# A three-layer graph convolution on one core: the first projection as fp32 matmuls, and the splits of x moved into hop 1

## The reference, cut to what matters

```python
def _tagconv(x, src, dst, norm, W, b):
    out = x @ W[0]
    h = x
    for k in range(1, K + 1):            # K = 3
        msg = norm[:, None] * h[src]
        h = jax.ops.segment_sum(msg, dst, num_segments=x.shape[0])
        out = out + h @ W[k]
    return out + b

h = jax.nn.relu(_tagconv(x, src, dst, norm, W1, b1))
h = jax.nn.relu(_tagconv(h, src, dst, norm, W2, b2))
out = _layernorm(x + _tagconv(h, src, dst, norm, W3, b3))
```

## Time and profile before

| | |
|---|---|
| median of 3 runs | 1251.7 us (1251.23 to 1251.88) |
| span of the profiled execution | 1250.4 us |
| TensorE busy | 1224.4 us (98%) |
| GpSimd, vector engine, ScalarE busy | 850.6, 629.7, 397.2 us |
| TensorE on the chain that ended last | 88% |
| TensorE matmuls at L1405 | 4104, 944.8 us |

### The profile page before, as it was taken

How to read it: one execution, slowest core, us unless ns; L and a number is a source line. 1 busy time by engine, 2 the same in 40 slices (tenths; PEclk the granted TensorE clock), 3 DMA queues, 4 the chain that set the end, 5 groups by cost and what they waited for, 6 DMA issues and landing times.

```text
span 1250.4 us, 19518 instructions
## 1 busy us (share of the span) xinstructions
PE 1224.4 (98%) x7413; PEld 610.2 (49%) x7413; DVE 629.7 (50%) x1552; ACT 397.2 (32%) x916; POOL 850.6 (68%) x937
## 2 busy tenths in 40 slices
PE   5999999999999999999999999999999999999997
PEld 4655554444444444444444454444444544454444
DVE  7876664444455555433443345555433433345655
ACT  6676774422233331111221122222111111112222
POOL 8677775777477755776577657773777477747773
PEclk8999999999999999999999999999999999999999
DMA  5343443544255553444354435553444344435553
GB/s 182 111 124 107 115 124 101 156 135 135 79 142 157 146 126 104 131 130 125 108 156 132 122 97 150 149 149 94 131 130 128 102 129 130 131 92 151 153 162 93
DMA packets 110070, 160.05 MB, mean 128 GB/s; under 512 B 43719, under 2 KB 82225, under 8 KB 109970
## 3 DMA queue, kind: packets, MB, share of 16 engines
q0 software_dynamic: 40480, 110.54, 31.6%
q1 hardware_dynamic: 69416, 48.13, 12.8%
q10 hardware_dynamic: 74, 0.05, 0.0%
HBM read 120.51 MB, written 32.10 MB: 122 GB/s over the span
## 4 chain that ended last, share of the span: by engine, by line
PE 88%; POOL 5%; DVE 3%; issue 2%; ACT 1%; DMA 1%; POOLq 0%; DVEq 0%; ACTq 0%
PE pb L1405 65%; PE pb L1266 6%; POOL GB L942 4%; PE pb L1319 4%; PE pb L1268 3%; PE pb L1285 3%; PE pb L1161 2%; PE pb L1410 1%; PE pb L1291 1%; PE pb L1383 1%; PE pb L1194 0%; DVE V L1744 0%; POOL gT L825 0%; DMA GB<-vh,KS 0%; DVE gT L1503 0%
## 5 line engine op out<-in xcount | busy, mean ns | idle before, releaser
L942 POOL DMA_INDIRECT GB<-vh,KS x837 | 807.9, 965 | 371.2 <-issue 246.2
L1405 PE MATMUL pb<-V,A 128*128 128x512 f16 x4104 | 944.8, 379 | 0.0
L1405 PEld LDWEIGHTS pb<-V,A 128*128 128x128 fp8e4 x4104 | 395.3, 98 | 429.5 <-issue 5.2
L1789 DVE SCALAR_TENSOR_TENSOR pb<-pb,cst,t 128x256 f32<-128x256 f32 (+1 forms) x200 | 97.7, 488 | 357.8 <-ACT t L1120 357.8
L1120 ACT ACTIVATE t<-pb,cst 128x256 f32<-128x256 f32 (+1 forms) x224 | 105.2, 469 | 441.8 <-PE pb L1410 398.0
L1266 PE MATMUL pb<-Whl,gT 128*128 128x512 f16 x384 | 134.2, 380 | 1.2 <-DVE gT L1730 1.2
L1761 DVE SCALAR_TENSOR_TENSOR V<-V,pb 128x256 f16<-128x256 f16 (+1 forms) x200 | 83.8, 421 | 82.1 <-ACT V L1090 81.5
L1090 ACT ACTIVATE V<-pb 128x256 f16<-128x256 f32 (+1 forms) x200 | 75.9, 383 | 127.3 <-DVE pb L1789 127.2
L1268 PE MATMUL pb<-Whl,gT 128*128 128x256 f16 x384 | 104.7, 273 | 0.0
L1632 DVE TENSOR_REDUCE stat<-V 128x1 f32<-128x256 f16 x225 | 91.3, 412 | 0.2
L1780 DVE TENSOR_REDUCE ast<-A 128x1 f32<-128x610 uint8 x100 | 77.8, 778 | 0.0
(11 more groups left out here) (227 smaller groups left out, 687.8 us busy)
## 6 DMA issues: line engine op xcount, KB each, us to landing
vh<-V SPq DMA_DIRECT2D x216, 128.0 KB
GB<-vh,KS POOLq DMA_INDIRECT x837, 2.8
xr<-in_x SPq DMA_DIRECT2D x24, 128.0 KB, 3.0
out<-g SPq DMA_DIRECT2D x24, 128.0 KB, 1.9
xr<-in_W SPq DMA_DIRECT2D x22, 128.0 KB, 2.4
V<-in_xt SPq DMA_DIRECT2D x5, 512.0 KB, 6.1
gT<-w SPq DMA_TRANSPOSE x46
V<-in_xt SPq DMA_DIRECT2D x1, 640.0 KB, 3.8
```

The source lines that it names most:

```text
L942: pool.indirect_dma_start(GB[:, slot, :], None, vh[vbuf[(L, k + 1)]][:, :], bass.IndirectOffsetOnAxis(ap=KS[:, p:p + 1], axis=0))\
L1405: mm = pe.matmul(acc[:, :], A8[:, a, t * P:(t + 1) * P], src[:, a, :], start=False, stop=(n == NT - 1), skip_group_check=True)
L1789: dve.scalar_tensor_tensor(hi, hi, cst[0:r, 1, t:t + 1], lt, ALU.mult, ALU.add).then_inc(S["s_d1"], 1)
```

## The change

The first projection takes x and W3 as they were loaded, in fp32: two matmuls a tile in place of six. W3's split is gone, and the scale factor SW with it. Eight tiles and not six are projected early; 8 and 9 stand between builds, 10 to 24 are woven into target 0. The splits of x for tiles 0 to 7 stay early; those of tiles 8 to 24 are done one tile at a time, at item `("A", i)` that `split_behind` gives: one tile at i = 1, 4, 5, 6, 8, 10, 11, 13 and 15, and two at 7, 9, 12 and 14. The second keys move to items 1 and 2, their transposes behind dense target 3, their copies to item 5, the tail keys from item 2 to item 6.

```diff
-AHEAD = 9
-BEHIND_P = {6: (4, 5), 7: (6,)}
-KEYED = {("V", 0, 3, 5): 0, ("V", 0, 3, 15): 1}
+AHEAD = 10
+BEHIND_P = {8: (4, 5), 9: (6,)}
...
-SPLITS = {("V", 0, 3, 8): 3, ("V", 0, 3, 11): 4, ("V", 0, 3, 14): 5}
-PAIRED = (6, 6, 2, 2)
+PAIRED = (6, 6, 2, 2, 0, 0, 1, 1)
+XS = 2
+KEYED, KEPT = {1: 0, 2: 1}, 5
...
+def split_behind(i):
+
+    asked = {}
+    for n, it in enumerate(it for it in schedule() if it[0] in "SP" and it[1:3] == (0, 2)):
+        if it[0] == "P" and it[3] in dense(0, 2):
+            at = DENSE.index(it[3])
+            asked.setdefault("next", at + 1)
+            asked["next"] = at + 1
+        elif it[0] == "S":
+            asked[it[3]] = asked.get("next", 0)
+    return [t for t in range(XC[XS], NT) if asked[t] - 2 == i]
...
@@ scalar @@
-            act.activation(Whl[:, 0, :, 3, 0:F], W3, ACT.Copy, scale=SW).then_inc(S["s_whi"], 1)
...
+                    if it[1] == KEPT:
+                        kept(1)
+                    for t in split_behind(it[1]):
+                        x_high(t, t + 1)
@@ tensor @@
-                pe.wait_ge(S["s_xd"], next(c for c in range(len(XC)) if t < XC[c]))
+                pe.wait_ge(s_x[next(c for c in range(len(XC)) if t < XC[c + 1])], 16)
...
                 for c in range(2):
-                    for half, part in ((0, slice(0, F)), (0, slice(F, 512)), (1, slice(0, F))):
-                        mm = pe.matmul(acc, gT[:, t, c, half, 0:r], Whl[:, 0, c, 3, part],
-                                       start=(c == 0 and half == 0 and part.start == 0),
-                                       stop=(c == 1 and half == 1), skip_group_check=True)
+                    at = F * t + P * c
+                    mm = pe.matmul(acc, xT[:, at:at + r], W3[:, c, :], start=(c == 0), stop=(c == 1),
+                                   skip_group_check=True)
...
-            for t in range(6):
+            for t in range(len(PAIRED)):
                 first_projection(t)
...
+                if k == 2:
+                    pe.wait_ge(S["s_xd"], split_at(t))
...
+                if (L, k, t) == (0, 2, DENSE[KEPT - 2]):
+                    swapped(1)
@@ vector @@
-            for c in range(2):
-                x_low(c)
+            for c in range(XS):
+                x_low(XC[c], XC[c + 1])
...
-                    if it[1] == 2:
+                    if it[1] in KEYED:
+                        keyed(1, KEYED[it[1]])
+                    if it[1] == KEPT:
+                        kept(1)
+                    if it[1] == KEPT + 1:
                         tail_keys()
+                    for t in split_behind(it[1]):
+                        x_low(t, t + 1)
```

More of the change, by code:

```diff
@@ L630, in first_acc, with x_part @@
             return bank[bank_of[pe_no[(0, 3, t)]]][0:P if t < NT - 1 else HALF, at:at + F]
-        def x_part(c, half):
-            a, b = XC[c], XC[c + 1]
+        def x_part(a, b, half):
             return (gT[:, a:b, :, half, :], xT[:, F * a:F * b].rearrange("p (t c n) -> p t c n", c=2, n=P))
@@ L641, in bass_tag_gnn_layernorm @@
         names = ("s_h s_w s_b s_cst s_cnt s_idx s_wk s_ki s_kt s_kb s_ka s_hs s_oh s_up s_og s_gc s_vis s_ev "
[L642 removed]
+                 "s_ob s_dw s_pl5 s_rl s_wq s_wi s_deg s_dg s_sq s_cs s_xh s_xd s_pj s_pm s_sm s_c0 s_c5 s_hs64 s_ps s_a1 s_d1 s_a2 "
                  "s_v s_g s_tp s_th s_tl s_z s_ln s_sd s_o s_dd s_st s_ck s_pk s_flag s_turn s_lp "
[L644 removed]
+                 "s_ld s_pl s_at s_at0 s_sg s_dl s_pc s_yg s_yh s_yl s_ps5 s_cp5 s_k5 s_t5 s_s5 s_gm s_nr").split()
         S = {n: sem(n) for n in names}
@@ L950, in _, with x_high @@
             act.activation(lnb[:, 0, 0:1], ones16[:, 0:1], ACT.Sign)
-            act.wait_ge(S["s_w"], 16)
-            act.activation(Whl[:, 0, :, 3, 0:F], W3, ACT.Copy, scale=SW).then_inc(S["s_whi"], 1)
-            def x_high(c):
-                act.wait_ge(s_x[c], 16)
-                if XC[c + 1] > 17:
+            def x_high(a, b):
+                act.wait_ge(s_x[next(c for c in range(len(XC)) if a < XC[c + 1])], 16)
+                if 10 <= a < 16:
                     act.wait_ge(S["s_ki"], QK // KQ)
-                if XC[c + 1] > 21:
                     act.wait_ge(S["s_k5"], 2)
-                high, xs = x_part(c, 0)
+                high, xs = x_part(a, b, 0)
                 act.activation(high, xs, ACT.Copy, scale=SX).then_inc(S["s_xh"], 1)
@@ L977, in scale_start @@
                 act.activation(acc, acc, ACT.Copy, scale=cst[:, 7, t:t + 1]).then_inc(S["s_pm"], 1)
-            for c in range(3):
-                x_high(c)
+            for c in range(XS):
+                x_high(XC[c], XC[c + 1])
             for u in range(2):
@@ L1270, in project, with split_at @@
                 return mm
+            def split_at(t):
+                if t < XC[XS]:
+                    return next(c for c in range(len(XC)) if t < XC[c])
+                return XS + 1 + [a for i in range(len(DENSE)) for a in split_behind(i)].index(t)
             def started(k, t):
@@ L1494, in _, with x_low @@
                               ALU.is_gt).then_inc(S["s_og"], 1)
[L1495 to L1502, removed]
+            parted = 0
+            def x_low(a, b):
+                nonlocal parted
+                parted += 1
+                dve.wait_ge(S["s_xh"], parted)
+                (high, xs), (low, _) = x_part(a, b, 0), x_part(a, b, 1)
                 dve.scalar_tensor_tensor(low, xs, SX, high, ALU.mult, ALU.subtract).then_inc(S["s_xd"], 1)
@@ L1537, in keyed @@
                 ai, bi = part(wf.bitcast(I32), 2 * n * c), part(wf.bitcast(I32), 2 * n * c + n)
-                kf, sq, dl = part(wf, 2 * n * c), part(wf, 2 * n * c + n), part(gf, n * c)
+                kf, sq, dl = part(wf, 2 * n * c), part(wf, 2 * n * c + n), part(gf, n * c) if c == 0 else part(wf, 0)
                 if not half:
@@ L1543, in keyed @@
                     return
+                if c > 0:
+                    link(dve.tensor_tensor(dl, G[:, KQ * c:KQ * (c + 1), 1, :],
+                                           thr[:, 1, KQ * c:KQ * (c + 1)].unsqueeze(2).broadcast_to([P, KQ, P]),
+                                           ALU.subtract))
                 link(dve.tensor_tensor(sq, dl, dl, ALU.mult))
@@ L1703, in _ @@
                     onehots(MARKS[was])
[L1704 to L1711, removed]
                 if was == ("V", 0, 3, NT - 3):
@@ L1776, in _ @@
                         for l in (0, 1) if L == 1 else (2,):
-                            largest(12 * NT + l, Whl[:, l % 2].rearrange("p c k n -> p (c k) n")[:, :, 0:F], AX.XY)
+                            largest(12 * NT + l, Whl[:, l % 2, :, 0:4 if l else 3, 0:F], AX.XYZ)
                     if k < 3 and L > 0 and nam < NAM:
```

27 lines of the change are left out of this document (10 added, 17 removed).

## The result

Median 1271.46 us (five runs, 1270.75 to 1273.65) against 1251.38 beside it (1251.19 to 1251.88): 1.0163 times the time before, interval 1.0152 to 1.0173, or **+20.1 us**. The forecast was +14.5, 1266 us in 1255 to 1272. The profiled execution took 1271.46 us with a span of 1269.7, so its span is 19.3 longer than that of before. The execution of before that was profiled took longer than its median: with the 1.8 us that lie between span and time here, its span of 1250.4 makes some 1252.2 us, an estimate. So differences of the two profiles are 0.5 to 0.8 us smaller than differences of medians.

A forecast was written before the change was run, and what follows sets the result against it. TensorE, busy 98% of the span, was taken to bound the kernel. Front and sweep +5.7 and hop 1 +8.8 made +14.5 us, added to the 1251.7 us median: 1266 us, range 1255 to 1272.

The forecast's parts named there:

- The front: Start of the kernel up to target 0's sweep; front and sweep together were to lose 5.7 us.
- Hop 1: Vector engine's splits wait for ScalarE's, delaying the next one-hots; TensorE waits for them, +8.8 us (6 to 12).
- The price of an fp32 projection: TensorE time of one fp32 tile: 0.88 us at full clock, 1.76 at half; bounds 0.44 and 1.45.
- The end is near 18 us: In the front, the eight early fp32 projections start at 8.83 us and end near 18 us.
- free: Early projections cost nothing, since L1207 waits for the vector engine's degrees until 20.72 us.
- The sweep starts at 39.8: Tiles 8 and 9 wait for V5's and V7's banks at half clock; sweep starts at 39.8 instead of 35.25, 4.5 us late.
- 22.0 + 1.4: Target 0's sweep: 22.0 us of work with fp32 tiles, plus 1.4 us of new waits at tiles 14 and 17.
- ready at R + 2.28: Hop 1: from R, the start of ScalarE's last copy (L1022), the next one-hots are ready 2.28 us later.
- the distances g: Hop 1: time from R until TensorE's first build wants the one-hots; three values, 0.58, 1.24 and 2.09 us.
- Clock stays up: Rival: shorter TensorE gap in the front keeps the full clock; front only +2.6, 1263 us; chance 0.12.
- Weight loads show: Rival: fp32 weight loads not hidden behind the stream, 15 x 0.57 = 8.6 us more, 1275 us; chance 0.05.
- Faster: Rival: freed vector and scalar engines pull V5 and V7 forward; front gives -4, 1249 us; chance 0.06.

The follow-up runs named there:

- banks: Changed kernel with one bank list reordered: tile 8 takes PSUM bank 2, tile 9 bank 0, tile 10 bank 1; 1265.55 us.
- filler: Changed kernel plus 20 unread fp32 products in TensorE's gaps of the front, written to an idle PSUM bank; 1268.71 us.
- low_later: Changed kernel with each low split of x on the vector engine one item later than ScalarE's high split; 1261.62 us.
- best: Changed kernel with ScalarE's high splits one item earlier, tile 8 in bank 2, tile 9 in bank 0, GpSimd's edge gather behind enlarging V7; 1253.67 us.
- half_k: Changed kernel where woven tiles 10 to 24 make only one of their two fp32 calls, so the output is wrong; 1267.69 us.
- both: Changed kernel with the edits of low_later and banks together; 1255.59 us.
- best_fill: best plus ten unread fp32 products in TensorE's gaps ahead of 28 us; 1254.83 us.

## Why the prediction came out as it did

The direction, both places and both mechanisms were right. It was 5.6 us low: 1.2 in the front, 3.6 in hop 1, and the rest is the 0.3 behind hop 1 and the 0.5 by which medians and profiles differ.

**The price of an fp32 projection** was right. Four records a tile, two to a call, and in the sweep the matmul that follows starts 0.87 us behind the tile's start (41.78 to 42.65). The changed kernel's L1202, ns min/median/max:

```profile
L1202 PE MATMUL pb<-g,V x100: 377/379/796, 8.8 to 59.2; 128*128 128x256 f32 x96, 128*64 128x256 f32 x4
L1202 PEld LDWEIGHTS pb<-g,V x100: 133/190/338, 8.8 to 59.0; 128*128 128x128 f32 x96, 128*64 128x64 f32 x4
```

The weight loads are hidden. A record's length (379) is not its price: the records overlap, 0.22 us apart at full clock. The Trainium skill (FP8 and Floating Point Precision, TensorE Precision Notes) counts four passes for true FP32; 0.88 us for 8 times 0.11 agrees.

**The front.** "The end is near 18 us" held (17.62), and so did "free". "The sweep starts at 39.8" was 0.8 early: tile 8 at 31.14 (I had 30.9), tile 9 at 36.15 (35.55), tile 10 at 40.60 (39.8). banks shows that the bank was the cause; the half clock, which I had put into the same steps, is 2.1 us of it by filler. The sweep and its waits, 22.0 + 1.4, took 63.93 − 40.60 = 23.3, and the new waits at the two places named were 0.49 and 0.75. The 0.4 us that I took off for a full clock at 20.7 us were not seen: the counting products L1214 came at 21.36 and not at 20.72, since the gathered table came later (below), and ScalarE took V0 at 24.23 where before it was 24.04. So 0.8 − 0.1 + 0.4 = 1.1 us too little. Part of that is luck of the execution and not a step that was wrong: low_later, with the same front, had L1214 at 20.53 and tile 10 at 39.86, almost the forecast, and yet ended target 0 0.17 us later, since its clock stayed at half until 43.5.

**Hop 1** is the step that was mis-sized: "ready at R + 2.28". In the rows above R is 71.06 and the build starts at 73.68: **R + 2.62**. ScalarE's split ends 0.75 behind R, not 0.62; from there (71.81) to the vector engine's start 0.11 us, and from the one-hots' end (73.53) to TensorE's build 0.15, where I had 0.05 for all handoffs: 0.13 + 0.11 + 0.15 − 0.05 = 0.34. I had written that 0.1 us of the chain is worth 1 us here; 0.34 is then 3.4 us, measured 3.0. The list of items, as the step in the ends of the targets:

```
item        1     4     5     6     7     8     9     10    11    12    13    14    15
forecast    1.70  0.82  0     1.04  1.38  0.19  0.45  0.16  1.04  0.53  1.04  0.50  0
measured    2.03  1.12  0     1.37  1.66  0.44  0.64  0.44  1.30  0.77  1.31  0.77  0
```

The sums are 8.8 and 11.9; the transposes (0.4) and 0.1 at target 1 make 12.4. Every item that has a wait has 0.2 to 0.35 us more, eleven times, and the two without one have none. The places, the parity of the builds and, to 0.1 us or so, the distances g were right; the three small terms of the chain were the error.

**The second keys** cost 0.44 us, the four transposes, back in TensorE's queue at 89 us, inside target 4. I had taken them off the sweep and put them "behind target 3" without adding them to the hop, so this is a slip of 0.4 us in the sum.

**The rivals.** "Clock stays up" fell: the gap was 3.75 us and not 5.3, and the clock still dropped at 22.4 us, 4.8 us behind the last early matmul (4.7 before). "The front alone" fell with the 12 us of the hop. "Weight loads show" fell with 0.87 us a tile. "Faster" fell because V5 still came at 31.1.

**What the kernel is left with.** The fp32 tiles cost TensorE 0.21 us more than f16 ones, and the vector and scalar time they free showed no gain in any run, in a kernel that is 98% TensorE. With both waits mended, best is still 2.3 us slower than before. What part of this is the sweep's stream and what the V tiles was not split further; half_k says that something over half of the stream's price reaches the end.

## What to carry to other kernels

Two engines that make the halves of one product meet at the place in program order where each of them stands, not where there is time: if one of them runs ahead, the wait falls on the work queued behind its half. Look for the engine that is behind, put its half one step earlier (or the other's one step later), and price such a chain with every start and handoff in it, since it is paid once per item: here 0.34 us left out became 3 us. When a reordering of tiles goes round a ring of buffers, read who used each buffer last: here a change of one list gave back 5.6 us, part of it by the clock that came back earlier.

## What the runs showed of the hardware

- The granted clock fell from 2.4 to 1.2 GHz 4.8 us behind the last matmul of the early work in the changed kernel (4.7 in before, 5.1 in low_later), but only 2.5 us behind it in the run named both and 2.2 in best_fill, so the distance is no constant. It came back at 39.5 us, when TensorE had been at work with short gaps since 36, and in low_later, with the same front, only at 43.5; unread products in the gaps of filler held it at 1.00 all through. The time that gave back was 2.1 us in the changed kernel; shortening the half clock in before gave 0.3, since there V tiles pace.
- fp32 matmuls of 256 columns leave two records a call, 379 ns each, 0.22 us apart at full clock ((42.65 − 41.78)/4) and 0.47 at half ((33.01 − 31.14)/4); their weight loads add nothing to be seen in the 0.87 us of a tile.
- L1214 stands between 20.45 us (half_k) and 21.48 (banks) in the profiles of kernels that put nothing in the gap ahead of it, and the causes differ. In the changed kernel the five issues of the gather on GpSimd were longer (1.95 and 1.79 us for the first two, 1.42 and 1.86 before), and the last ended 0.57 us later. In banks they were short (1.95 and 0.96), but a cast of the vector engine at 14.39 us lasted 1.95 us (others of its line 0.29). The start of target 0's sweep moves with it, but its end moved by 0.2 us between the changed kernel and low_later and by 0.7 between banks and the run both. A forecast from one profile has that error in it.
- The profiled executions of two kernels (low_later, best_fill) lost 1.9 and 1.3 us by target 17, at 190 to 198 us, with TensorE standing 0.9 us and more for a gather that landed late; the others lost 0.4 at most there. Why those two was not looked into.
